# Building the query and key stacks of the last layer with one matmul instead of two, from tiles that hold high and low parts side by side

## What is computed

```python
def _L3_gnn_ref(x, adj_matrix, bond_matrix, Wq, bq, Wk, bk, Wv, bv, Wo, bo, seq_len):
    ...
    q, k, v = (proj(Wq, bq), proj(Wk, bk), proj(Wv, bv))
    scores = jnp.einsum('bhqd,bhkd->bhqk', q, k) * SCALE
    mask = (adj_matrix + bond_matrix)[:, None, :, :]
    scores = scores * mask
    attn = jax.nn.softmax(scores, axis=-1)
    ctx = jnp.einsum('bhqk,bhkd->bhqd', attn, v)
    ...
x = _layernorm(x + _L0_gnn_ref(x, adj, L0_gnn_W), axis=-1)
x = _layernorm(x + _L1_gnn_ref(x, adj, ...), axis=-1)
x = _layernorm(x + _L2_gnn_ref(x, adj, ...), axis=-1)
x = _layernorm(x + _L3_gnn_ref(x, adj, adj, ..., 1024), axis=-1)
```

## Time and profile before

| what | value |
|---|---|
| time, median of 3 runs | 3142.06 us (3141.99 to 3142.89) |
| the profiled execution: its own time | 3141.49 us |
| the profiled execution: span of the core | 3139.7 us |
| granted TensorE clock, mean | 0.992 |
| PE busy | 3023.2 us (96%) |
| DVE busy | 2090.6 us (67%) |
| ACT busy | 1724.4 us (55%) |
| POOL busy | 448.6 us (14%) |

### The profile page before, as it was taken

One profiled execution on the slowest core, in us unless ns is written; L12 is line 12 of the kernel. 1 busy time (PEld: TensorE's weight loads), 2 busy tenths in 40 slices (PEclk: granted clock), 3 DMA queues, 4 the chain that ended last, 5 costly groups with the idle time before them and its releaser, 6 DMA issues.

```text
span 3139.7 us, 71133 instructions
## 1 busy us (share of the span) xinstructions
PE 3023.2 (96%) x28188; PEld 2645.5 (84%) x28188; DVE 2090.6 (67%) x4060; ACT 1724.4 (55%) x3048; POOL 448.6 (14%) x1666
## 2 busy tenths in 40 slices
PE   6999999999999999999999999999999999999999
PEld 5988789877898788987889877898778987789877
DVE  4637976379762797627976389753887538874388
ACT  3525855258542684526844278442784337853377
POOL 0101211012110121101211012111121111211112
PEclk9999999999999999999999999999999999999999
DMA  5022131121321213202133021330213302133010
GB/s 218 30 79 65 49 145 54 57 70 44 144 77 37 67 52 135 96 22 67 49 135 108 12 71 44 134 108 14 69 52 125 108 14 72 49 125 108 24 42 19
DMA packets 145270, 234.50 MB, mean 75 GB/s; under 512 B 12839, under 2 KB 113964, under 8 KB 144940
## 3 DMA queue, kind: packets, MB, share of 16 engines
q1 hardware_dynamic: 144940, 229.96, 22.3%
HBM read 120.86 MB, written 83.89 MB: 65 GB/s over the span
## 4 chain that ended last, share of the span: by engine, by line
PE 87%; DVE 7%; ACT 3%; issue 2%; SPq 1%; POOL 1%; DMA 0%; DVEq 0%; POOLq 0%; ACTq 0%
PE ps L506 16%; PE ps L508 16%; PE ps L507 16%; PE ps L734 15%; PE ps L724 9%; PE ps L752 8%; PE ps L605 1%; DVE t_lo L1228 1%; PE ps L765 1%; PE ps L564 1%; PE ps L595 1%; DVE al_area L1371 1%; DVE u_hi L1385 1%; ACT t_hi L931 1%; PE ps L705 0%
## 5 line engine op out<-in xcount | busy, mean ns | idle before, releaser
L1525 DVE CUSTOM_DVE_ANT_0 r<-ps,adjn 128x1024 f32<-128x1024 f32 x512 | 620.7, 1212 | 18.9 <-DVE xr L1572 10.3
L1172 ACT ACTIVATE r<-r,nmax 128x1024 f32<-128x1024 f32 x512 | 584.8, 1142 | 23.0 <-POOL nmax L498 22.3
L506 PE MATMUL ps<-u_hi,t_hi 128*128 128x256 f32 x2048 | 588.6, 287 | 0.6
L508 PE MATMUL ps<-u_hi,t_lo 128*128 128x256 f32 x2048 | 579.3, 283 | 0.0
L507 PE MATMUL ps<-u_lo,t_hi 128*128 128x256 f32 x2048 | 578.9, 283 | 0.0
L734 PEld LDWEIGHTS ps<-ident,r 128*128 128x128 f32 x4096 | 462.5, 141 | 115.4 <-issue 77.4
L734 PE MATMUL ps<-ident,r 128*128 128x128 f32 x4096 | 536.8, 274 | 7.2 <-DVE pt L1541 7.0
L1541 DVE COPY pt<-ps 128x512 f32<-128x512 f32 x512 | 352.9, 689 | 93.4 <-PE ps L734 73.8
L931 ACT ACTIVATE pt<-ps 128x512 f32<-128x512 f32 x512 | 304.0, 594 | 176.5 <-PE ps L734 158.2
L506 PEld LDWEIGHTS ps<-u_hi,t_hi 128*128 128x128 f32 x2048 | 391.5, 191 | 4.0 <-DVE t_lo L1228 4.0
L507 PEld LDWEIGHTS ps<-u_lo,t_hi 128*128 128x128 f32 x2048 | 391.4, 191 | 0.0
(11 more groups left out here) (165 smaller groups left out, 5237.2 us busy)
## 6 DMA issues: line engine op xcount, KB each, us to landing
adjn<-in_adj SPq DMA_DIRECT2D x64, 512.0 KB, 3.4
t_spill<-t_hi SPq DMA_DIRECT2D x64, 512.0 KB, 5.9
t_spill<-t_lo SPq DMA_DIRECT2D x64, 512.0 KB, 6.0
t_hi<-t_spill SPq DMA_DIRECT2D x32, 1024.0 KB, 5.4
t_lo<-t_spill SPq DMA_DIRECT2D x32, 1024.0 KB, 8.1
xn<-in_x SPq DMA_DIRECT2D x16, 512.0 KB, 4.2
x_spill<-xn SPq DMA_DIRECT2D x64, 128.0 KB, 1.7
q_stack<-u_hi SPq DMA_DIRECT2D x64, 128.0 KB, 2.5
```

The source lines that it names most:

```text
L506: pe.matmul(dst, a_hi, b_hi, start=first, stop=False, skip_group_check=check)
L508: return pe.matmul(dst, a_lo, b_hi, start=False, stop=last, skip_group_check=check)
L1172: act.activation(r[:, s % RSLOTS, :], r[:, s % RSLOTS, :], ACT.Exp, bias=nmax[:, s % 4:s % 4 + 1], accum_out=prow[:, qt % 2, h:h + 1]).the ...
L1525: dve.tensor_tensor_reduce(out=r[:, s % RSLOTS, :], in0=ps[:, 2 * (s % 2):2 * (s % 2) + 2, :].rearrange("p a c -> p (a c)"), in1=adjn[:, q ...
```

## The change

- **One matmul for each copy.** `qk0_hi` and `qk0_lo` become one tile `qk0`, in which a block holds the high parts of two heads in 64 partitions and their low parts in the other 64. A copy is one matmul with 96 columns of a new `placer` (12 identity blocks and no zeros).
- **Split read-outs.** To fill `qk0`, each ft = 0 part is read out in two instructions of 64 partitions on ACT and two on DVE. Those of DVE write to other partitions than they read.
- **Order and banks.** The projections stand in a new order (`QK`), in which the ft = 1 parts come earlier and values 0 after the sixth part; they use banks 2 and 3 beside 6 and 7 (`WIDE`). The copies stand in the order query half 0, key half 0, key half 1, query half 1 (`COPIES`); the last four are done inside step 0 of the loop into banks 4 to 7, before values 1, which waits in step 1 for them.
- **DMAs.** SP issues the eight low-part DMAs first, then the sixteen high-part ones. The slots of `pt_0` are turned by four, so that the first three copies of DVE lie over `u_lo`: DVE waits for the low parts alone at its first copy and for the rest at its fourth. ACT no longer waits for the DMAs.

```diff
-    COPIES = [(h, m, half) for half in range(HALVES) for m in range(2) for h in range(G)]
+    COPIES = [(h, m, half) for m, half in ((0, 0), (1, 0), (1, 1), (0, 1)) for h in range(G)]
...
-    QK = [(1, 0, 0), (1, 1, 0), (0, 0, 0), (0, 1, 0), (1, 0, 1), (1, 1, 1), (0, 0, 1), (0, 1, 1)]
+    QK = [(1, 0, 0), (1, 1, 0), (0, 0, 0), (1, 0, 1), (1, 1, 1), (0, 1, 0), (0, 1, 1), (0, 0, 1)]
+    COPIES_AHEAD = {6: (0, 1), 7: (2, 3, 4, 5)}
+    COPIES_NEXT, COPIES_LATE = range(6, 3 * G), range(3 * G, 4 * G)
+    QK_HI = [sum(2 - ft for ft, m, half in QK[:k + 1]) for k in range(len(QK))]
...
-                [("qk", part) for part in QK[:4]] + [("values", 0)] + [("qk", part) for part in QK[4:]] +
+                [("qk", part) for part in QK[:6]] + [("values", 0)] + [("qk", part) for part in QK[6:]] +
...
+    WIDE = {("qk", part): bank for part, bank in zip(QK, (6, 7, 2, 3, 6, 7, 6, 7))}
+    WIDE["values", 0] = 2
+    PR_BANK = [WIDE[unit] if unit in WIDE else 6 + n % 2 for n, unit in enumerate(PR_ORDER)]
+    PR_BEFORE = [max([m for m in range(n) if PR_BANK[m] == PR_BANK[n]], default=-1) for n in range(PR_UNITS)]
...
-        placer = sb("placer", [P, (4 * G + 2) * HD], F32R)
+        PLACED = (64, 0, 0, 64, 64, 0, 96, 32, 32, 96, 96, 32)
+        placer = sb("placer", [P, len(PLACED) * HD], F32R)
...
+        def qk0_place(m, half, heads, low):
+
+            at = (2 * (1 - m) + heads) * N + half * 512
+            first = 64 * (1 - heads if low else heads)
+            return qk0[first:first + 64, at:at + 512]
+
...
             if half == 0:
-                return pt_0[:, u % P0SLOTS, :, :]
+                return pt_0[:, (u + TPH) % P0SLOTS, :, :]
...
-            return ps[0:STACK, ACC + n % 4 if n < 3 * G else TP + n % 2, :]
+            return ps[0:STACK, ACC + n % 4 if n < 3 * G else TP + n % 4, :]
...
+                for n, stack in enumerate((q_stack, k_stack)):
+                    sp.wait_ge(pr_free, nth(b, PR_UNITS, pr["qk", (1, n, 1)] + 1))
+                    for g in range(G):
+                        part = 2 if n == 0 else 0
+                        sp.dma_start(f32(stack[HD * part:HD * (part + 1), G + g, :]),
+                                     f32(u_lo[HD * g:HD * (g + 1), n * N:(n + 1) * N])).then_inc(lo_stacked, 16)
...
-                if 4 <= n < 3 * G or n >= 3 * G + 2:
-                    copied(b, n - (4 if n < 3 * G else 2))
...
-                if m == 0:
-                    pe.matmul(dst, block(2, 3), qk0_hi[:, 0, at], start=True, stop=False)
-                    last = pe.matmul(dst, block(0, 3), qk0_lo[:, 0, at], start=False, stop=True)
...
+                if 4 <= n < 3 * G:
+                    copied(b, n - 4)
+                if n == 2:
+                    pe.wait_ge(pr_free, nth(b, PR_UNITS, pr["values", 0] + 1))
+                at = (2 * (1 - m) + h // 2) * N + half * 512
+                first = (h % 2) * 6 + (h // 2) * 2 + (1 - m)
+                pe.matmul(copies_bank(n), placer[:, first * HD:(first + 3) * HD], qk0[:, at:at + 512],
+                          start=True, stop=True).then_inc(copies_full, 1)
...
-                if u == 0:
-                    copied(b, 3 * G - 2)
-                    copied(b, 3 * G - 1)
-                if u < G:
-                    copied(b, 3 * G + u)
+                if u < 2:
+                    copied(b, 2 * G + 2 * u)
+                    copied(b, 2 * G + 2 * u + 1)
...
+                    if s == 1:
+                        copied(b, 4 * G - 2)
+                        copied(b, 4 * G - 1)
...
+            for k, row in enumerate(PLACED):
+                last = copy(placer[:, k * HD:(k + 1) * HD], ident[:, row:row + HD])
...
-                        if u == 0:
-                            for g in range(G):
-                                act.wait_ge(stacked[g], nth(b, 16 * 6, 16 * 6))
...
+                    for heads in range(2) if ft == 0 else ():
+                        rows = slice(64 * heads, 64 * (heads + 1))
+                        dve.wait_ge(qk_hi, nth(b, 12, QK_HI[k] - 1 + heads))
+                        last = dve.scalar_tensor_tensor(out=qk0_place(m, half, heads, True), in0=ps[rows, PR_BANK[n], :],
+                                                        scalar=cols[rows, 2 + m, ft:ft + 1],
+                                                        in1=f32(qk0_place(m, half, heads, False)), op0=ALU.add,
+                                                        op1=ALU.subtract)
...
                         if u == 0:
+                            dve.wait_ge(lo_stacked, nth(b, 16 * 2 * G, 16 * 2 * G))
+                        if u == 3:
                             for g in range(G):
-                                dve.wait_ge(stacked[g], nth(b, 16 * 6, 16 * 6))
+                                dve.wait_ge(stacked[g], nth(b, 16 * 4, 16 * 4))
```

More of the change, by code:

```diff
@@ L286, in nth, with qk_place @@
             return b * per + n
[L288 to L292, removed]
+        def qk_place(staged, m, half):
+            return staged[:, m * N + half * 512:m * N + (half + 1) * 512]
         def copies_place(n):
@@ L888, in _ @@
                         transpose_x_late(b, 3, n)
-                    if n == 4:
+                    if n == 2:
+                        pe.wait_ge(acc_free, nth(b, 3 * NT, 3 * NT))
+                    if n == 6:
                         project_pairs(b, "values", W_V, xt_wait(b, 3), range(1))
-                    if n == 7:
-                        for k in range(G):
-                            stack_copies(b, k)
+                    for k in COPIES_AHEAD.get(n, ()):
+                        stack_copies(b, k)
                     pe.wait_ge(tp_free, nth(b, TP_UNITS, x_ready(3, TPH * half + TPH - 1)))
@@ L900, in _ @@
                     last.then_inc(pr_full, 1)
-                for n in range(G, 3 * G + 2):
+                for n in COPIES_NEXT:
                     stack_copies(b, n)
@@ L907, in _ @@
                     if s == 0:
-                        for n in range(3 * G + 2, 4 * G):
+                        for n in COPIES_LATE:
                             stack_copies(b, n)
+                    if s == 1:
+                        copied(b, 4 * G - 2)
+                        copied(b, 4 * G - 1)
                     if 1 <= s < PAIRS:
@@ L942, in _ @@
             copy(ones_2[:, :], ones[:, 0:2])
[L943 to L948, removed]
-                    copy(placer[:, (4 * h + k) * HD:(4 * h + k + 1) * HD], ident[:, HD * h:HD * (h + 1)])
+            for k, row in enumerate(PLACED):
+                last = copy(placer[:, k * HD:(k + 1) * HD], ident[:, row:row + HD])
+            last.then_inc(set_act, 1)
             for k in range(2):
@@ L1149, in _ @@
                     act.wait_ge(pr_full, nth(b, PR_UNITS, n + 1))
-                    act.activation(qk_place(part, u_hi, qk0_hi), ps[:, PR + n % 2, :], ACT.Identity,
-                                   bias=cols[:, 2 + m, ft:ft + 1]).then_inc(qk_hi, 1)
-                stacks_copied(range(G, 4 * G, 2))
+                    if ft == 1:
+                        act.activation(qk_place(u_hi, m, half), ps[:, PR_BANK[n], :], ACT.Identity,
+                                       bias=cols[:, 2 + m, ft:ft + 1]).then_inc(qk_hi, 1)
+                    for heads in range(2) if ft == 0 else ():
+                        rows = slice(64 * heads, 64 * (heads + 1))
+                        act.activation(qk0_place(m, half, heads, False), ps[rows, PR_BANK[n], :], ACT.Identity,
+                                       bias=cols[rows, 2 + m, ft:ft + 1]).then_inc(qk_hi, 1)
+                stacks_copied(COPIES_NEXT[::2])
+                stacks_copied(COPIES_LATE[::2])
                 for s in range(UNITS + 14):
@@ L1504, in _ @@
                         x_late_transposed(b, 3, k)
-                    if k == 4:
+                    if k == 6:
                         values(0)
-                    if k == 7:
-                        stacks_copied(range(1, G, 2))
+                    stacks_copied(COPIES_AHEAD.get(k, ())[1::2])
                     ft, m, half = part
                     n = pr["qk", part]
-                    dve.wait_ge(qk_hi, nth(b, 8, k + 1))
-                    dve.scalar_tensor_tensor(out=qk_place(part, u_lo, qk0_lo), in0=ps[:, PR + n % 2, :],
-                                             scalar=cols[:, 2 + m, ft:ft + 1], in1=f32(qk_place(part, u_hi, qk0_hi)),
-                                             op0=ALU.add, op1=ALU.subtract).then_inc(pr_free, 1)
-                stacks_copied(range(G + 1, 3 * G + 2, 2))
+                    if ft == 1:
+                        dve.wait_ge(qk_hi, nth(b, 12, QK_HI[k]))
+                        dve.scalar_tensor_tensor(out=qk_place(u_lo, m, half), in0=ps[:, PR_BANK[n], :],
+                                                 scalar=cols[:, 2 + m, ft:ft + 1], in1=f32(qk_place(u_hi, m, half)),
+                                                 op0=ALU.add, op1=ALU.subtract).then_inc(pr_free, 1)
```

(9 more changed lines are left out.)

42 lines of the change are left out of this document (16 added, 26 removed).

## The result

The changed kernel takes 3132.55 us (median of nine runs, 3131.32 to 3135.30), the kernel before 3142.06 (nine runs, 3141.32 to 3144.11): ratio 0.9971, 95% interval 0.9961 to 0.9981. It is faster, by 9.5 us and not by the 18.6 that I had forecast, and lies outside my range. The profiled execution took 3132.17 us.

What follows compares the result with a forecast made beforehand. PE bounds the kernel (busy 3023 of 3140 us), but DVE paces the loop's first steps. Each element gains 2.10 - 0.51 + 0.66 = 2.25, eight 18.0, setup 0.6, together 18.6: 3123.5 us, range 3117 to 3130.

Steps and rivals of the forecast that it cites:

- PE's clock falls: Rival: half clock from scores 0 to the first transposes in each element, 4.65 us later; 3160 us, chance 0.04.
- Setup: Before the elements: building `placer` with 12 shorter copies in place of 13 saves 0.58 us, kept by PE.
- Banks and order: Projection stage: the wait ahead of values 0 goes; late transposed rows cost about 0.1 us.
- single matmuls: Stack copies: 16 matmuls fewer per element, 29.8 us of PE in all, but not that much gain.
- split read-outs: Projection parts: four more instructions each on ACT and DVE per element, each half priced as a whole, 0.75 us on DVE.
- DVE's chain: End of the projection stage: DVE's halves and copies set scores 0, which comes 2.10 us earlier per element.
- Late copies: Loop start: they delay values 1, losing 0.51 us before the mark (first context matmul behind first projection).
- DMAs: Stack DMAs ahead of the first copy to `pt`: no element waits, 0.66 us gained for each on average.
- Halves that stream: Rival: split read-outs on DVE follow at 0.67 us, mark 0.41 earlier per element; 3120.2 us, chance 0.25.
- Dearer halves: Rival: split read-outs cost 0.69 on ACT, 0.90 on DVE, mark 0.70 later; 3129.1 us, chance 0.12.
- my main case: The whole sum, each half read-out costing a whole one: 3123.5 us with some 2 either side, chance 0.50.
- The DMA wait stays: Rival: `pt` still waits for stack DMAs, as more transfers move at once; loses 5.3 us, 3128.8, chance 0.05.

Runs made afterwards that it cites:

- Experiment 2: Changed kernel with ten unread matmuls added per element where PE waits, ahead of copies 7, 10, 11 and scores 0: 3124.35 us.
- experiment 1: Changed kernel with every copy's matmul issued twice into the same bank, putting the removed PE work back: 3138.64 us.
- experiment 3: Kernel before with one matmul per copy in place of two, low parts of heads 0 to 3 left out: 3141.95 us.
- experiment 4: Changed kernel with DVE and ACT again waiting for all 24 stack DMAs ahead of their first copy to `pt`: 3134.01 us.
- experiment 5: Experiment 2's kernel with five copies read out by ACT in place of DVE, other late banks and filler counts: 3118.92 us.
- experiment 8: Experiment 5's kernel plus twelve unread matmuls at each element's start: 3112.76 to 3113.72 us in three executions, 6878.53 in the fourth.
- experiment 11: The kernel of experiment 8 run once more, unchanged: 3112.49 us, ratio 0.9906 to the kernel before.

## Why the prediction was wrong

- **The clock of PE is the step that failed.** I had it as a rival at 0.04, "PE's clock falls", and wrote against it that the clock stood at full "through the waits of before". Those waits were shorter and fewer: one of 0.31 us between the last projection and scores 0, where the change has 0.49, 0.54 and 0.83. My own working had PE at work for only 1.4 us of 4.3 there, and I gave the fall no place in the sum. It fell in seven of eight elements. I had priced it at 4.65 us for each, with half clock up to the first transposes; it lasted until 283.3 in element 0 only and cost 2.0 us there, 0.97 to 1.05 in six, nothing in element 1: 8.2 us in all. Experiment 2 takes just this away and lands at 3124.35; experiment 1 takes it away by putting the removed work back. Halved matmuls alone did not bring the fall at scores 0 (experiment 3); the longer waits of the whole change did.
- **Setup.** Forecast 0.58 earlier; the first projection starts 1.0 us later (256.95 against 255.96), 1.6 off. Building `placer` did get shorter (0.60 us); the 1.1 us are the transposes at half clock. Other executions have this start at 255.7 to 258.3, so it is spread more than effect.
- **The other terms.** Banks and order, single matmuls, split read-outs and DVE's chain: scores 0 at +19.85 against 19.7; DVE's two pairs of halves at the end of the chain took 1.54 to the next instruction where I had 1.50. Late copies: mark 37.26 where the clock stayed, against 37.2. DMAs: no element waits. That leaves 0.08 x 8 = 0.6 us. Together 8.2 + 1.6 + 0.6 = 10.4 us too much; 9.3 were missing in the spans, and the other 1.1 came in at the starts of elements, where the half clock lasted less than in the profile before (23.9 us in all against 30.7). That I count as spread.
- **The rivals.** Halves that stream: no, 1.51 us for two. The rule of the Trainium skill (VectorE: DVE Perf Modes, section on two Vector instructions with no wait between them), that an instruction which starts in another quadrant is held until the earlier ones have finished, agrees with the trace: 0.75 us each, and the next starts behind the end. Dearer halves: on ACT yes, 0.71 us apart where that rival had 0.69 and my main case 0.59; on DVE no, 0.76 to 0.79 to the next instruction and not 0.90. As DVE ends the chain, ACT's part cost little: scores 0 came 0.14 us behind my working, not 0.7. The DMA wait stays: no; by experiment 4 the waits alone would not have brought it back.
- **Open.** Why the same waits bring the clock down in seven elements and not in element 1 (in experiment 4 they do it in all eight): no run here tells.

## What to carry to other kernels

Where PE is the bound and a change shortens its work in a stage paced by other engines, PE's waits there get longer, and its clock may fall and take back a part of the gain just behind them: ask of each removed matmul what PE does in its place. A few matmuls that nobody reads, put exactly where PE waits, cost nothing in experiment 2 and kept the clock (8 us in the stage, some 3 at the starts of elements); one too many, as in experiment 5, stands in the way itself. A read-out split by partitions costs twice; here it cost 10.8 us, more than the 5.3 that I had given the DMAs.

## What the hardware showed beyond that

One execution of the version in experiment 8 took 6878.53 us where seven others took 3111 to 3114. DVE's busy time is nearly the same (2183 us, 2097 in experiment 11), but PE's matmuls of 512 columns stand 0.62 us apart in place of 0.233 for the first five elements, and 0.45 in the last three:

```profile
599.83 0.78 PE L524 MATMUL ps<-xt_hi,w_hi 128*128 128x512 f32 x1
600.45 0.78 PE L525 MATMUL ps<-xt_lo,w_hi 128*128 128x512 f32 x1
601.06 0.78 PE L526 MATMUL ps<-xt_hi,w_lo 128*128 128x512 f32 x1
```

The view of this execution gives a granted clock of 1.00, but its page has no row of the clock at all, unlike those of all other runs here: nothing was recorded, and 1.00 says nothing. Whether PE's clock was lower is open, and so is the cause; it did not come again in four executions.
